# Two-layer decoder: the expert layers' row norm on three engines, the constant's products in four column groups, and waits per constant

## The reference, cut to what matters

```
mu, var = mean(x), var(x)                                   # per row
xn = (x - mu) * rsqrt(var + 1e-5) * gamma + beta
probs = softmax(xn @ Wr + br);  scores, idx = top_k(probs, 2)
full_e = relu(xn @ W1[e] + b1[e]) @ W2[e] + b2[e]           # 256 -> 1024 -> 256
c_e = relu(b1[e]) @ W2[e] + b2[e];  c_total = sum_e c_e     # one row of 256 for all rows of x
output = sum over the 2 choices of score * (full_e - c_e + c_total)
x = layernorm(x + (x + output))
```

## Time and profile before

| what | us |
|---|---|
| median of 3 runs | 1652.29 (1652.24 to 1653.98) |
| the profiled execution's own time | 1652.67 |
| its span | 1650.7 |
| busy: PE, DVE, ACT, POOL | 1430.9, 1213.4, 1019.9, 902.1 |
| m0's block begins, m1's block begins (first instruction) | 678.60, 1375.70 |

### The profile page before, as it was taken

The page is one execution under the profiler, slowest core; times in us unless marked ns, Lnnn a source line. Parts: engine busy times, 40 slices in busy tenths (PEclk is TensorE's granted clock), DMA queues, the critical chain, the costliest instruction groups (busy, mean ns, idle before and its releaser), DMA issues. The chain is left out here.

```text
span 1650.7 us, 29045 instructions
## 1 busy us (share of the span) xinstructions
PE 1430.9 (87%) x9778; PEld 1177.5 (71%) x9778; DVE 1213.4 (74%) x2550; ACT 1019.9 (62%) x2476; POOL 902.1 (55%) x898
## 2 busy tenths in 40 slices
PE   4778999999999999599999999078899867999991
PEld 3656777777777776489999999035555536999991
DVE  5677766666666666575999999479898961868874
ACT  4666565565565565225778777357777843458883
POOL 3664554444444445106999997038778761068761
PEclk8899999999999999679999999579999995999996
DMA  4000000000000000355565663354343412237664
GB/s 153 26 27 8 27 8 8 2 8 8 1 8 8 2 1 1 110 211 182 203 240 203 239 208 135 119 180 145 126 139 119 141 51 77 77 100 258 245 191 165
DMA packets 53828, 171.60 MB, mean 104 GB/s; under 512 B 13546, under 2 KB 22708, under 8 KB 45236
## 3 DMA queue, kind: packets, MB, share of 16 engines
q1 hardware_dynamic: 44852, 145.63, 24.8%
q0 software_dynamic: 8832, 24.13, 4.7%
HBM read 151.12 MB, written 18.61 MB: 103 GB/s over the span
## 5 line engine op out<-in xcount | busy, mean ns | idle before, releaser
L307 POOL TENSOR_TENSOR a_pexp<-a_pexp,a_rsum 128x384 f32<-128x384 f32 (+1 forms) x320 | 246.0, 787 | 302.5 <-DVE a_rsum L524 302.5
L397 ACT ACTIVATE a_pexp<-a_ps,a_nmax 128x384 f32<-128x384 f32 (+1 forms) x320 | 181.2, 566 | 171.6 <-DVE a_nmax L520 171.0
L1556 PE MATMUL m_ps<-m_xT,m_w1s 128*128 128x256 f32 x1848 | 278.7, 288 | 2.0 <-DVE m_xT L1366 1.1
L1574 PE MATMUL m_ps<-m_w2s,m_hs 128*128 128x256 f32 x1848 | 271.7, 283 | 2.8 <-DVE m_hs L1394 1.6
L1556 PEld LDWEIGHTS m_ps<-m_xT,m_w1s 128*128 128x128 f32 x1848 | 244.5, 191 | 5.3 <-DVE m_xT L1366 1.3
L1574 PEld LDWEIGHTS m_ps<-m_w2s,m_hs 128*128 128x128 f32 x1848 | 240.5, 189 | 5.0 <-issue 2.7
L520 DVE TENSOR_REDUCE a_nmax<-a_ps 128x1 f32<-128x384 f32 (+1 forms) x320 | 154.1, 523 | 70.9 <-PE a_ps L621 69.9
L1796 POOL TENSOR_TENSOR s_hc<-s_h,s_bc_rows 128x1024 f32<-128x1024 f32 x64 | 150.8, 2358 | 80.1 <-DVE s_h L2038 79.8
L1022 POOL DMA_INDIRECT m_xrow<-table,m_row_from x92 | 98.5, 1071 | 156.2 <-DVE m_row_from L1308 130.2
L2038 DVE TENSOR_TENSOR_SCAN s_h<-s_dps,s_inp 128x512 f32<-128x512 f32 x128 | 149.3, 1210 | 0.0
L637 PE MATMUL a_ps<-a_ident,a_pexp 128*128 128x128 f32 x896 | 144.2, 273 | 3.4 <-ACT a_pT L256 3.0
(11 more groups left out here) (336 smaller groups left out, 3385.8 us busy)
## 6 DMA issues: line engine op xcount, KB each, us to landing
s_bc_rows<-s_bc_table SPq DMA_DIRECT2D x64, 512.0 KB, 3.7
m_w<-in_down SPq DMA_DIRECT2D x29, 1024.0 KB, 7.0
m_w<-in_up SPq DMA_DIRECT2D x23, 1024.0 KB
m_w<-in_up SPq DMA_DIRECT2D x24, 512.0 KB, 4.5
m_w<-in_down SPq DMA_DIRECT2D x24, 512.0 KB, 3.4
m_w<-results SPq DMA_DIRECT2D x4, 1024.0 KB, 8.8
m_fin<-results SPq DMA_DIRECT2D x4, 1024.0 KB, 7.9
tokens<-in_x SPq DMA_DIRECT2D x8, 256.0 KB, 6.8
```

The source lines that it names most:

```text
L307: nc.gpsimd.tensor_tensor(pexp[:, r, 0:n], pexp[:, r, 0:n], rsum[:, r:r + 1].to_broadcast([128, n]), ALU.mult).then_inc(normed, 1)
L397: nc.scalar.activation(pexp[:, r, 0:n], ps_s[score_bank(u)][:, 0:n], ACT.Exp, bias=nmax[:, r:r + 1], accum_out=sums[:, r:r + 1]).then_inc( ...
L1556: last = nc.tensor.matmul(ps_hid[ft % RING], w1s[wb][wp][:, k, ft * 128:(ft + 1) * 128], xT[:, j % 2, xp, k, :], start=(k == 0 and wp == 0 ...
L1574: last = nc.tensor.matmul(ps_y[j % 2][:, s, :], hs[hp][:, ft % RING, s * 128:(s + 1) * 128], w2s[wb][wp][:, ft, :], start=(ft == 0 and s = ...
```

## The change

In both layers the one semaphore of SP's constants becomes one for each use (`s_rows[0]` gamma, `s_rows[1]` beta, `s_router`, `s_bias`), and gamma and beta are issued ahead of the router's weights and bias. POOL makes the identity right after its memset; PE begins when it is there (`s_ident`) and waits for the router's weights at the first router product and for POOL's other constants at `count_slots`. In the norm DVE keeps statistics, subtract-and-multiply and the reciprocal; the multiplication by the reciprocal root goes to ACT (`scale_row`), the addition of beta to POOL. ACT takes the square root and the four scalings of the next group between its copies of the present one. The constant's products are made with 32 columns of weights instead of 128, hidden part `ft` in column group `ft % 4`, summed in four groups of 32 partitions (`ps_parts`); DVE copies these sums out after `slot_rows` (after all eight experts), and PE adds the four groups with one product by 1/32 (`share`) and the second biases with another (`constant_rows`), now after the transposes of tiles 0 and 1.

```diff
--- before.py
+++ after.py
...
+GCONST = 11 + (b_down is not None)
 CT_RING = 3
...
     ct_new = sb("ct_w", [128, FT, D])
+    ct_parts = sb("ct_parts", [128, D])
+    share = sb("share", [128, 128])
     ct_w = [w2[:, 1], w1[:, 1].rearrange("p k f -> p (k f)").rearrange("p (f d) -> p f d", d=D), ct_new[:]]
...
 ps_h, ps_t, ps_r = ps[0:4], ps[6], ps[7] if shared else ps[3]
-ps_ct = ps[7][:, D:2 * D]
+ps_ct, ps_parts = ps[7][:, D:2 * D], ps[2][:, 0:D]
 ps_lg, ps_rank, ps_tot, ps_id = ps_r[:, 0:TT * E], ps_r[:, TT * E:2 * TT * E], ps_r[:, 2 * TT * E:3 * TT * E], ps_r[:, 3 * TT * E:3 * TT * E + HALVES]
...
-s_const = sem("s_const"); s_gconst = sem("s_gconst")
+s_rows = [sem(f"s_rows{n}") for n in range(2)]; s_router = sem("s_router"); s_bias = sem("s_bias"); s_ident = sem("s_ident"); s_gconst = sem("s_gconst"); s_centred = sem("s_centred"); s_scaled = sem("s_scaled"); s_inverse = sem("s_inverse")
 s_xn = sem("s_xn"); s_tr = sem("s_tr"); s_ev = sem("s_ev"); s_logit = sem("s_logit")
...
 s_ctw = [sem(f"s_ctw{b}") for b in range(4)]; s_ctb = sem("s_ctb"); s_ctm = sem("s_ctm")
-s_ctp = sem("s_ctp"); s_var = sem("s_var"); s_rstd = sem("s_rstd"); s_double = sem("s_double")
+s_ctp = sem("s_ctp"); s_parts = sem("s_parts"); s_ctr = sem("s_ctr"); s_var = sem("s_var"); s_rstd = sem("s_rstd"); s_double = sem("s_double")
 xrow_loaded = [sem(f"xrow_loaded{b}") for b in range(2)]
...
     def _(sp):
-        sp.dma_start(wr[:], w_router.rearrange("(k p) e -> p k e", p=128)).then_inc(s_const, 16)
-        if b_router is not None:
-            sp.dma_start(br[:], b_router.partition_broadcast(128)).then_inc(s_const, 16)
         if ln_rows is not None:
             for n in range(2):
-                sp.dma_start(bcast[:, n, :], ln_rows[n].partition_broadcast(128)).then_inc(s_const, 16)
+                sp.dma_start(bcast[:, n, :], ln_rows[n].partition_broadcast(128)).then_inc(s_rows[n], 16)
+        sp.dma_start(wr[:], w_router.rearrange("(k p) e -> p k e", p=128)).then_inc(s_router, 16)
+        if b_router is not None:
+            sp.dma_start(br[:], b_router.partition_broadcast(128)).then_inc(s_bias, 16)
         if b_down is not None:
...
     def _(pool):
-        nc.gpsimd.memset(ident[:], 0.0).then_inc(s_gconst, 1)
+        nc.gpsimd.memset(ident[:], 0.0).then_inc(s_ident, 1)
+        pool.wait_ge(s_ident, 1)
+        nc.gpsimd.affine_select(out=ident[:], in_=ident[:], compare_op=ALU.not_equal, fill=1.0, base=0,
+                                pattern=[[-1, 128]], channel_multiplier=1).then_inc(s_ident, 1)
         nc.gpsimd.memset(ones[:], 1.0).then_inc(s_gconst, 1)
...
         nc.gpsimd.iota(dump[:], [[128, HALVES]], base=2 * T + 2, channel_multiplier=1, allow_small_or_imprecise_dtypes=True).then_inc(s_gconst, 1)
-        pool.wait_ge(s_gconst, 10)
-        nc.gpsimd.affine_select(out=ident[:], in_=ident[:], compare_op=ALU.not_equal, fill=1.0, base=0,
-                                pattern=[[-1, 128]], channel_multiplier=1).then_inc(s_gconst, 1)
-
+        if b_down is not None:
+            nc.gpsimd.memset(share[:], 1.0 / 32).then_inc(s_gconst, 1)
+        pool.wait_ge(s_gconst, 9 + (b_down is not None))
         nc.gpsimd.affine_select(out=tri[:], in_=ones[:], compare_op=ALU.is_gt, fill=0.0, base=0,
...
+        if ln_rows is not None:
+            pool.wait_ge(s_rows[1], 16)
+            for t in range(TT):
+                pool.wait_ge(s_scaled, t + 1)
+                nc.gpsimd.tensor_tensor(xn_of(t), xn_of(t), bcast[:, 1, :], ALU.add).then_inc(s_xn, 1)
         for g in range(GROUPS):
...
+        def scale_row(t):
+            if t % GROUP == 0:
+                act_e.wait_ge(s_inverse, t // GROUP + 1)
+            act_e.wait_ge(s_centred, t + 1)
+            nc.scalar.activation(xn_of(t), xn_of(t), ACT.Copy, scale=rstd[:, t:t + 1]).then_inc(s_scaled, 1)
+
         for g in range(GROUPS):
-            if ln_rows is not None:
-                take_root(g, g + 1)
+            if ln_rows is not None and g == 0:
+                take_root(0, 1)
+                for t in range(GROUP):
+                    scale_row(t)
             for t in range(g * GROUP, (g + 1) * GROUP):
...
                 nc.scalar.copy(xT_r[:, t % 2, :, :], ps_h[t % 2][:, 0:KD * 128].rearrange("p (k n) -> p k n", k=KD)).then_inc(s_ev, 1)
+                if ln_rows is not None and t + GROUP < TT:
+                    if t % GROUP == 0:
+                        take_root(g + 1, g + 2)
+                    scale_row(t + GROUP)
             if shared and g == GROUPS // 2 - 1:
...
-        def inverse_root(g):
+        def inverse_root(g, done=None):
             norms[0] += 1
...
             cols = slice(g * GROUP, (g + 1) * GROUP)
-            link(nc.vector.reciprocal(rstd[:, cols], rstd[:, cols]))
-
-        dve.wait_ge(s_const, 16 * (1 + (b_router is not None) + 2 * (ln_rows is not None)))
+            taken = nc.vector.reciprocal(rstd[:, cols], rstd[:, cols])
+            if done is None:
+                link(taken)
+            else:
+                taken.then_inc(done, 1)
+
         for g in range(GROUPS):
...
                     dve.wait_ge(s_tr, (g - 1) * GROUP)
+                if g == 0:
+                    dve.wait_ge(s_rows[0], 16)
                 for t in range(g * GROUP, (g + 1) * GROUP):
-                    last = nc.vector.scalar_tensor_tensor(xn_of(t), x[:, t, :], mv[:, t, 0:1], bcast[:, 0, :], ALU.subtract, ALU.mult)
-                link(last)
-                inverse_root(g)
-                for t in range(g * GROUP, (g + 1) * GROUP):
-                    nc.vector.scalar_tensor_tensor(xn_of(t), xn_of(t), rstd[:, t:t + 1], bcast[:, 1, :], ALU.mult, ALU.add).then_inc(s_xn, 1)
+                    nc.vector.scalar_tensor_tensor(xn_of(t), x[:, t, :], mv[:, t, 0:1], bcast[:, 0, :], ALU.subtract, ALU.mult).then_inc(s_centred, 1)
+                inverse_root(g, s_inverse)
         def softmax_scores():
             dve.wait_ge(s_logit, TT)
-            dve.wait_ge(s_gconst, 13)
+            dve.wait_ge(s_gconst, GCONST)
             logits = ps_lg.rearrange("p (t e) -> p t e", e=E)
             if b_router is not None:
+                dve.wait_ge(s_bias, 16)
                 link(nc.vector.tensor_tensor(prob[:], logits, br[:].unsqueeze(1).to_broadcast([128, TT, E]), ALU.add))
...
             if t == 0:
-                dve.wait_ge(s_ctm, E + 1)
+                dve.wait_ge(s_ctr, 1)
             dve.wait_ge(s_double, t // GROUP + 1)
...
             slot_rows()
+            dve.wait_ge(s_ctm, E)
+            nc.vector.tensor_copy(ct_parts[:], ps_parts).then_inc(s_parts, 1)
         for c in range(FT):
...
         pe.sem_inc(h_used, FT + 1)
-        pe.wait_ge(s_gconst, 13)
-        pe.wait_ge(s_const, 16)
+        pe.wait_ge(s_ident, 2)
...
             for ft in range(FT):
-                last = nc.tensor.matmul(ps_ct, b1_all[:, e, ft:ft + 1].to_broadcast([128, 128]), ct_w[e % CT_RING][:, ft, :],
-                                        start=(e == 0 and ft == 0), stop=False)
+                c = slice(ft % 4 * 32, ft % 4 * 32 + 32)
+                last = nc.tensor.matmul(ps_parts[c, :], b1_all[:, e, ft:ft + 1].to_broadcast([128, 32]), ct_w[e % CT_RING][:, ft, :],
+                                        start=(e == 0 and ft < 4), stop=(e == E - 1 and ft >= FT - 4))
             last.then_inc(s_ctm, 1)
...
             pe.wait_ge(s_ev, t + 1)
+            if t == 0:
+                pe.wait_ge(s_router, 16)
             for k in range(KD):
...
             pe.wait_ge(s_hot, 1)
+            pe.wait_ge(s_gconst, GCONST)
             hot_cols = hots[:].rearrange("p t e -> p (t e)")
...
             last.then_inc(s_numbers, 1)
+
+        def constant_rows():
+            pe.wait_ge(s_parts, 1)
+            nc.tensor.matmul(ps_ct, share[:], ct_parts[:], start=True, stop=False)
+            nc.tensor.matmul(ps_ct, ones[0:E, :], b2s[:], start=False, stop=True).then_inc(s_ctr, 1)
...
                 constant(e)
-            nc.tensor.matmul(ps_ct, ones[0:E, :], b2s[:], start=False, stop=True).then_inc(s_ctm, 1)
             pe.wait_ge(s_from, 1)
...
         transposes(1)
+        if not shared:
+            constant_rows()
         for ft in range(AHEAD):
...
         for j in range(TILES):
...
```

## The result

The changed kernel takes 1657.56 us (median of 13 runs, 1655.46 to 1661.98), the kernel before, beside it on the same chip, 1652.29 (13 runs, 1646.59 to 1658.06). The ratio is 1.003, 95% interval 1.0019 to 1.0041: slower by 3 to 7 us, where 0.8 less was forecast. The time lies above the predicted range. The profiled executions took 1656.95 (span 1655.0) and 1652.67, 4.3 apart.

A forecast was written before the change was run, and what follows sets the result against it. PE was taken to bound m0's tile loop (100.00 of 100 us busy). Terms: -0.1 - 3.4 + 0.9 + 2.8 - 1.0 = -0.8 us, from 1652.67 to 1651.9, or 1651.5 from the median; stated 1651.7, 8-in-10 range 1647.0 to 1655.2.

The forecast's parts named there:

- Part 3: Before m0's loop: after expert 7, DVE's copy and eight low halves, then tile 0's split at 747.1 against 750.55, -3.4 us.
- Part 4: Behind m0's split: `constant_rows` adds 0.9 us, and the tile loop starting at 1.2 GHz loses 2.8 us.
- Part 2: Constant's products before m0's loop: an expert takes 0.9 or 1.7 us, `numbers_of_slots` 7.4 at 1.2 GHz, experts end at 741.6.
- Part 1: m0's norm: rows start 3.3 us earlier, but group 2 waits for group 0's store until 695.7; worth -0.1 us.
- Part 5: Waits by use in m1: first router product at 1378.0 against 1379.03, -1.0 us.
- The premise: Time gained or lost ahead of m0's PE-bound tile loop, or of m1's tiles, reaches the end unchanged.
- The slow rival: Before m0's loop: column groups run one after another, DVE's copy delays the split to 754.0; +3.4 us, 1655.7, chance 0.14.

The follow-up runs named there:

- e2: Changed kernel with POOL's two 128x1472 products waiting until DVE has made tile 0's eight low halves; ratio 0.9996 to the kernel before, m0 357.4 us.
- e7: Changed kernel with POOL's two 128x1472 products in four pieces each, same work; ratio 1.0011 to the kernel before, m0 357.1 us.
- e1: Changed kernel with DVE's copy of the constant's sums moved behind tile 0's eight low halves; ratio 0.9998 to the kernel before, m0 355.0 us.
- e5: The changed kernel once more, unchanged, on another chip; ratio 1.0046 to the kernel before, m0 360.0 us.
- e10: Changed kernel with first constant loads behind the second store, DVE's copy behind the low halves, tile 1's weights issued after its gathered rows; ratio 0.9975 to the kernel before.
- e9: The kernel before, unchanged, as a run of its own and profiled again; ratio 1.0, m0 355.5 us.
- e6: Changed kernel with 10 and 12 unused f32 products on PE around tile 0's transposes, ahead of the loop; ratio 1.0019 to the kernel before, m0 355.9 us.
- e14: Changed kernel with unused f32 products behind expert 0 (5) and ahead of `numbers_of_slots` (6); ratio 1.0021 to the kernel before, m0 358.2 us.
- e13: Kernel before with waits by use alone: norm on DVE, constant undivided; ratio 0.9992 to the kernel before, m0 353.5 us.
- e3: Changed kernel with the constant undivided as before, norm on three engines and waits by use kept; ratio 0.9989 to the kernel before, m0 354.8 us.
- e12: Changed kernel with the constant undivided as before and the three first down-weight loads behind the norm's second store; ratio 0.9963 to the kernel before, m0 351.5 us.
- e8: Changed kernel with the three first 1 MB down-weight loads issued behind the first store; ratio 1.0049 to the kernel before, m0 361.5 us.

## Why the prediction was wrong

**Part 3, the copy and the halves: the step that failed.** It said that behind expert 7 come the copy, 0.5, and the eight halves, "4.9 us", split of tile 0 at 747.1. Expert 7 and the copy were on time, 740.8 against 741.6. The halves took 9.8 us, from 741.15 to 750.97. Their price came from the earlier trace rows, where they ran while POOL did nothing of the kind, and I moved them by some 5 us without asking what POOL does there; the two products stood in the trace of before at 743.86 and 746.60. The 4.9 us that they took beyond the forecast are the whole of 2 x (3.14 - 0.69). e2 keeps the two apart and has the price back, e7 cuts POOL's instruction and DVE's wait with it, e1 puts the copy behind the halves and they are fast too. So the collision is shown, by cause and by size. The forecast -3.4 became +0.5.

The same step had a second fault, hidden by the first: "Gathered rows are no longer last" is true for tile 0 only. e1 and e2 show PE held 5 to 6 us by the rows of tile 1, because the transposes of tile 1 stand ahead of tile 0's `up`. In both the split was early and PE waited for tile 1. Without the collision there would still have been no gain in m0. e2 comes nearest to the conditions of the forecast: its split is at 68.2, where 747.1 - 678.6 = 68.5 was forecast, and m0 is 357.4 and not 355.0. Of this 1.2 is the wait for tile 1's rows, whose transposes start 2.03 us behind the split instead of 0.82; the rest is the loop's cold start, 24 `up` records in 5.49 as in e5. In e1 the split came 4.2 earlier than forecast, and m0 at 355.0 was no shorter than before. I take it from e1's issue at 742.38, beside the gathers, that tile 1's weight loads, which came at 749.94 before, slow them. e10, where these loads wait for the rows, has 1.84 us left of it; but it moves two other things as well, so this is supported, not separated.

**Part 4, the clock and `constant_rows`: right, within a wide scatter.** Forecast 0.9 + 2.8 = 3.7. From the split to `weights_by_slot` the changed kernel is slower by 2.62 + 1.12 = 3.7, and e5 against e9 by 5.2, since there the clock rose later. The first term was mis-sized: it was priced at full clock, 4 x 0.215, although the next sentence put that stretch at 1.2 GHz, and the first `up` came 2.14 us behind the start of `constant_rows` (1.15 in e6, at full clock). What the rest of the cold start cost, 1.6, was below the 2.8 in the first pair, and 3.1, above it, in the second. e6 takes the low clock away and wins 2.7 to 4.0.

**Part 2, the column groups: right.** 1.94 and 1.04 us against 1.7 and 0.9; `numbers_of_slots` at 0.50, 6.99 against 7.4. e14 shows that this low clock costs 1.8 us at m0's end and not the 2.9 that it adds there, as POOL goes by the same numbers and the loads come next.

**Part 1, the norm: right in its wait, mis-sized.** -1.4 instead of -0.1, since group 2 came free of the store 1.4 earlier than I let it; from there the rows took what was forecast. e13 corrects what the part is made of: all of the gain comes from waiting for gamma and beta by use. Spreading the norm over three engines gives 0.9 to 1.9 of it back: the store holds group 2 in either form (e13, 1.61 us), and behind it the way over three engines is 1.4 longer.

**Part 5, m1:** -1.35 against -1.0, right.

**The premise.** "A microsecond gained or lost ahead of that loop therefore reaches the end unchanged" held for the losses. It did not for the gains: e3, e12 and e13 have their first `up` 2.4, 5.6 and 3.1 us earlier than the kernel before (its first profile for e3, e9 for the others), and m0 is only 0.0, 4.0 and 2.0 shorter; most of what is missing is the fall of the clock behind `weights_by_slot`, 1.4 to 1.5 us each time.

In m0 the forecast was +0.2 and the result +5.2. Of the difference 3.9 is Part 3, nothing Part 4 in this pair, and 0.9 the stops at m0's end, which are scatter. Part 1's 1.3 did not shift the split, which hung on numbers, the copy and POOL. The slow rival named the right place, the copy on DVE, and nearly the right time, 1655.7, but by another mechanism: it needed expert 7 at 748.6, and the groups did run side by side.

## What to carry to other kernels

When an instruction is moved in time, read what every other engine does in its new place, not only what feeds it: a DVE product with two operands, moved beside POOL's long elementwise instructions, costs 3.14 us instead of 0.69, and either the order or shorter POOL instructions takes that back. What is won ahead of a bound loop need not reach its end: measure at the end (e12 kept 4.0 of 5.6). A wait taken off the front of a queue (a store, a split, a gather) is worth only the distance to the next one, so look one tile further than the one that was late. When PE's work ahead of a bound loop is made shorter, price the loop's first microseconds at the lower clock, all of them.

## What the runs showed of the hardware

- DVE beside POOL. A 128x512 product with two tensor operands takes 0.69 us alone, 3.14 beside a 128x1472 product of POOL, and 1.28 beside pieces a quarter as long; POOL's goes from 2.66 to 2.98. Each time DVE's product ended some 0.55 us after the POOL product beside it, as if it waited for the whole of it with its own time behind. POOL's product that began before DVE's half took 2.66, and those that began while a half was still running 2.98 (e14). The norm has the same: beside POOL's additions four 128x256 subtractions of DVE took 2.21 instead of 1.67 (at 686.27 in the changed kernel). The Trainium skill (GPSIMD Engine Reference, 8. Key points) says that GpSimd shares its SBUF interfaces with VectorE and contends with its instructions that have two SBUF inputs; the trace agrees, and the size, 4.5 times, is this trace's.
- Column groups. Sixteen f32 records of 32 weight columns in four groups took 1.04 us where 128 columns took 3.62 (3.5 times), and 1.94 for 6.69 at the lower clock (3.4 times); two groups of 64 had given 1.8. The 2.38 times for three column tiles of the Trainium skill (TensorE: Matmul & The Clock Gate, Part 3) had been read as about 3.2 for four, an estimate; this case measured more.
- A store behind three loads of 1 MB in one queue let go of its tiles 7.3 us after its issue, and the later ones before the change landed in 2.6; in e8 the wait went to the store that was then behind them.
- The clock can fall inside a loop that keeps PE busy: to 0.50 for some 3 us right behind `weights_by_slot` in e3, e12 and e13, and not in the kernel before. No run here shows why.
- The kernel before took 1651.5 us on one chip and 1695.7 to 1697.4 on three others, with nearly all of the difference in m1 (275.0 us in the first profile, 316.9 in e9's). No run here shows why.
